# A local transformer on one core: probabilities divided by their sums on GpSimd, value products that give features by queries, the token shift by a transfer, and other orders of the engines' work

## What is computed

```python
def shift_tokens(t):
    a, s = jnp.split(t, 2, -1)
    s = jnp.pad(s, ((0, 0), (1, 0), (0, 0)))[:, :-1]
    return jnp.concatenate([a, s], -1)
...
def attn_layer(x, Wqkv, qs, ksc, Wo):
    q, k, v = jnp.split(x @ Wqkv, 3, -1)            # heads of 64
    ...
    q = l2norm(q) * qs
    k = l2norm(k) * ksc
    q = q * cos * scale + rotate_half(q) * sin * scale
    k = k * cos * inv + rotate_half(k) * sin * inv
    sim = jnp.einsum('bhwie,bhwje->bhwij', bq, bk2) * QK_SCALE
    sim = jnp.where(mask, -jnp.finfo(sim.dtype).max, sim)
    attn = jax.nn.softmax(sim, -1)
    out = jnp.einsum('bhwij,bhwje->bhwie', attn, bv2)
    return out @ Wo
...
for i in range(DEPTH):                              # 6
    x = attn_layer(shift_tokens(x), ...) + x
    x = ffn_layer(shift_tokens(x), ...) + x         # layer norm, 341 gated units, GELU
```

## Time and profile before

| | us |
|---|---|
| median of 3 runs | 2675.39 |
| range of the runs | 2669.9 to 2679.36 |
| the profiled execution | 2678.02 |
| its span, first to last instruction | 2676.1 |

### The profile page before, as it was taken

How to read it: one execution, slowest core, us unless ns; L and a number is a source line. 1 busy time by engine, 2 the same in 40 slices (tenths; PEclk the granted TensorE clock), 3 DMA queues, 4 the chain that set the end, 5 groups by cost and what they waited for, 6 DMA issues and landing times.

```text
span 2676.1 us, 103018 instructions
## 1 busy us (share of the span) xinstructions
PE 2507.1 (94%) x41090; PEld 1932.3 (72%) x41090; DVE 1977.9 (74%) x4815; ACT 1762.2 (66%) x3794; POOL 1492.9 (56%) x1917
## 2 busy tenths in 40 slices
PE   7879999999999999999999999999898978999898
PEld 5647677777767767777677767776677966899667
DVE  5777888888778788878788888887466877465564
ACT  5567777777777777777777777777344356333465
POOL 4567667666766766676667666775232146000472
PEclk9989999999999999999999999999799989899999
DMA  2200000111001100110011000000002000000022
GB/s 85 72 14 14 14 16 18 28 29 29 18 22 32 32 14 22 32 29 21 18 32 29 23 18 18 16 14 15 4 4 85 0 5 5 1 0 1 12 76 79
DMA packets 56280, 66.72 MB, mean 25 GB/s; under 512 B 25097, under 2 KB 30932, under 8 KB 55380
## 3 DMA queue, kind: packets, MB, share of 16 engines
q1 hardware_dynamic: 56148, 64.87, 8.7%
HBM read 38.23 MB, written 1.05 MB: 15 GB/s over the span
## 4 chain that ended last, share of the span: by engine, by line
PE 80%; DVE 6%; issue 5%; POOL 4%; ACT 3%; DVEq 1%; SPq 0%; POOLq 0%; DMA 0%; ACTq 0%
PE ps L795 13%; PE ps L900 6%; PE ps L816 6%; PE ps L809 6%; PE ps L880 5%; PE ps L843 5%; PE ps L922 4%; PE ps L857 3%; PE ps L1014 3%; PE ps L934 3%; PE ps L890 3%; PE ps L998 3%; PE ps L999 3%; ACT area L1190 2%; PE ps L738 2%
## 5 line engine op out<-in xcount | busy, mean ns | idle before, releaser
L1190 ACT ACTIVATE area<-ps 128x512 f32<-128x512 f32 (+3 forms) x1520 | 758.1, 532 | 415.9 <-PE ps L786 130.0
L1665 POOL TENSOR_TENSOR area<-area 128x512 f32<-128x512 f32 x384 | 482.2, 1277 | 7.9 <-DVE area L2164 7.9
L1687 POOL TENSOR_TENSOR area<-area,mx 128x512 f32<-128x512 f32 x192 | 200.2, 1043 | 491.1 <-DVE mx L2192 491.1
L795 PE MATMUL ps<-lw,area 128*128 128x512 f32 x768 | 414.1, 622 | 1.1 <-ACT area L1190 0.7
L1679 POOL TENSOR_TENSOR area<-area,rnq 128x512 f32<-128x512 f32 x384 | 393.2, 1046 | 7.5
L1313 ACT ACTIVATE area<-ps 128x512 f32<-128x512 f32 x384 | 227.4, 592 | 88.7 <-PE ps L795 88.6
L2162 DVE TENSOR_TENSOR area<-ps,table 128x512 f32<-128x512 f32 x384 | 261.0, 680 | 8.2 <-ACT area L1313 5.4
L2164 DVE TENSOR_TENSOR area<-ps,table 128x512 f32<-128x512 f32 x384 | 261.5, 681 | 0.0
L2143 DVE TENSOR_REDUCE ssq<-area 128x8 f32<-128x512 f32 x384 | 252.3, 677 | 2.4 <-ACT area L1313 1.5
L809 PE MATMUL ps<-ident,area 128*128 128x128 f32 x1536 | 218.6, 275 | 11.1 <-POOL area L1679 7.7
L809 PEld LDWEIGHTS ps<-ident,area 128*128 128x128 f32 x1536 | 180.7, 142 | 66.3 <-issue 54.3
(11 more groups left out here) (301 smaller groups left out, 5681.9 us busy)
## 6 DMA issues: line engine op xcount, KB each, us to landing
lvm<-area SPq DMA_DIRECT2D x384, 65.0 KB
lw<-in_wqkv SPq DMA_DIRECT2D x36, 256.0 KB
area<-in_moe_w SPq DMA_DIRECT2D x24, 256.0 KB, 2.8
lw<-in_wout SPq DMA_DIRECT2D x12, 256.0 KB
ctxT<-in_ctxT SPq DMA_DIRECT2D x64, 38.5 KB, 1.8
lw<-in_moe_w SPq DMA_DIRECT2D x8, 256.0 KB, 2.8
lw<-in_wff SPq DMA_DIRECT2D x6, 341.0 KB
lw<-in_moe_g SPq DMA_DIRECT2D x1, 1152.0 KB
```

The lines of the kernel that those rows point to most:

```text
L795: nc.tensor.matmul(banks[:, lb_qk[j], :], xsT[s], wqkv[w.p][:, j * 512:(j + 1) * 512], start=True, stop=True).then_inc(l_qk_ps, 1)
L1190: return nc.scalar.activation(dst, src, ACT.Identity if kw else ACT.Copy, **kw)
L1665: pool.tensor_tensor(QR[s][:, cols], QR[s][:, cols], RA[s][:, cols], ALU.add).then_inc(l_rsum, 1)
```

## The change

Five things change in the local transformer.

1. **Probabilities are divided before the value products.** `prob_sums` (VectorE, a reduction of 512 columns a half) and `inverse_sums` give the reciprocals, and `probs_normed` (GpSimd) multiplies the probabilities by them in place. `outputs` on VectorE is gone.
2. **`probs_values` gives features by queries.** Values are stationary (64 keys x 64 features), the transposed probabilities moving: for each pair of heads `c` query columns 0 to 63, 64 to 95 and 96 to 127, for the upper and the lower 64 rows in turn. That is 24 matmuls a half in two 64x64 tiles on the diagonal of the array, both into one PSUM bank. The result is already what `project` needs, so the transposes `outputs_T` on TensorE are gone; ScalarE copies straight from the products' bank.
3. **The shift of `y1` is a DMA transfer.** SyncE moves 127 rows x 64 features from `y1` one partition down into `ysh` beside it; VectorE reads columns 0 to 63 and 128 to 191 of `ysh`. `shift_back` and the constant `shift` are gone.
4. **New orders** of the work on TensorE, ScalarE, VectorE and GpSimd, and other PSUM banks. Values are projected by `values(*b, ...)`, no longer `values(*a, ...)`; the query and key blocks come in the order 2, 3, 0, 1; the transposes of queries and keys and the first scores of a unit now stand in its first step; `up` is split.
5. SyncE's transfers are issued per step by `stages`, with the shift behind the four middle transfers of the same unit.

```diff
             def probs_values(s, w, m):
...
                 for c in range(4):
-                    for n in range(4):
+                    for first, cols in ((0, 64), (64, 32), (96, 32)):
                         for odd in range(2):
-                            rows, out_rows = slice(64 * odd, 64 * odd + 64), slice(32 * n, 32 * n + 32)
-                            at = (4 * m + c) * S + 32 * n
-                            v = LVM[s][rows, 4 * m + c, :] if n == 2 else LV[s][rows, n // 2, 4 * m + c, :]
-                            last = nc.tensor.matmul(banks[out_rows, lb_pv[m][odd], c * 65:(c + 1) * 65],
-                                                    LPT[s][rows, at:at + 32], v, start=True, stop=True)
+                            rows = slice(64 * odd, 64 * odd + 64)
+                            at = c * S + first
+                            v = LVM[s][rows, 4 * m + c, 0:LD] if first == 64 else LV[s][rows, first // 64, 4 * m + c, 0:LD]
+                            last = nc.tensor.matmul(banks[rows, lb_pv[m], at:at + cols], v,
+                                                    LPT[s][rows, m * 512 + at:m * 512 + at + cols], start=True, stop=True)
...
-            def shift_back(s, w):
-                pe.wait_ge(l_y1, nth(0, w.it, s))
-                nc.tensor.matmul(banks[:, lb_shift, 0:64], ident[:, :], y1[s][:, 0:64], start=True, stop=True)
-                nc.tensor.matmul(banks[:, lb_shift, 64:128], shift[:, :], y1[s][:, 64:128],
-                                 start=True, stop=True).then_inc(l_sh_ps, 1)
...
+            def shifted_tokens(s, unit):
+                sp.wait_ge(l_y1, unit + 1)
+                sp.dma_start(ysh[s][1:S, D:D + 64], y1[s][0:S - 1, 64:D]).then_inc(l_sh_ps, 16)
+
+            def stages(a, b, c):
+                if a:
+                    middle_values(*a)
+                    shifted_tokens(*a)
...
+            def probs_normed(s, w, m):
+                if m == 1:
+                    pool.wait_ge(l_rc, nth(0, w.it, s, 2, 1))
+                P = heads8(LP[s], m)
+                pool.tensor_tensor(P, P, rc[s][:, 8 * m:8 * m + 8, None].to_broadcast([S, 8, 64]), ALU.mult).then_inc(l_o, 1)
...
+            def prob_sums(s, w, m):
...
+                V.tensor_reduce(sums[s][:, 8 * m:8 * m + 8], heads8(LP[s], m), AX.X, ALU.add).then_inc(l_psum, 1)
...
-            def outputs(s, w, m):
...
-                V.tensor_tensor(LO[s][:, m * 512:(m + 1) * 512].rearrange("p (c k e) -> p k c e", k=2, e=LD), pv(m)[:, :, :, 0:LD],
-                                per_head(rc[s][:, 8 * m:8 * m + 8])[:, :, :, None].to_broadcast([S, 2, 4, LD]), ALU.mult).then_inc(l_o, 1)
...
             def stages(a, b, c):
-                if a:
-                    values(*a, 0)
-                    values(*a, 1)
+                if b: values(*b, 0)
+                if a: tokens_T(*a)
+                if b: scores(*b, 1)
+                if a: queries_keys(*a, 2)
+                if b: values(*b, 1)
```

More of the change, by code:

```diff
@@ L554, in layer_and_next_weights @@
                             sp.dma_start(dst, src).then_inc(lw_loaded[p], 16)
-            layer(0)
+            stages((0, 0), None, None)
+            stages((1, 1), (0, 0), None)
+            with sp.Fori(0, IT - 1) as pr:
+                for s in range(G):
+                    three(s, pr * G + G + s)
             with sp.Fori(0, DEPTH // 2 - 1) as lp:
@@ L559, in _ @@
                 layer_and_next_weights(lp * 2 + 2, 1)
-            layer(DEPTH - 1)
+            with sp.Fori(0, IT) as pr:
+                for s in range(G):
+                    three(s, (DEPTH - 1) * B + pr * G + s)
+            stages(None, (1, DEPTH * B - 1), (0, DEPTH * B - 2))
+            stages(None, None, (1, DEPTH * B - 1))
             contexts(1)
```

357 lines of the change are left out of this document (174 added, 183 removed).

## The result

The changed kernel takes 2835.12 us (median of 4 runs, 2834.83 to 2839.52) against 2674.39 for the kernel before on the same chip: a ratio of 1.0601, 95% interval 1.058 to 1.0622. The prediction had the direction (slower) and was 102 us too fast: 2733 us, range to 2805.

What follows compares the result with a forecast made beforehand. TensorE, 94% busy, was taken as the bound. A step of 17.15 + 1.3 + 0.1 = 18.55 against 17.85 us, taken as +0.65, times 95 gave +62, drain -4: 2736, or 2733 us from the runs' median; range 2645 to 2805.

Steps and rivals of the forecast that it cites:

- What bounds the kernel, and that all lies in 95 steps: TensorE, 94% busy, bounds the kernel; the change lies wholly inside 95 local transformer steps of 17.85 us on average.
- Removed work, 1.46 us: TensorE's step loses two output transposes, 0.53 and 0.44 us, and the pair of shift matmuls, 0.49 us.
- Value products, 1.4 a half: In TensorE's step, 24 record pairs at 0.058 us take 1.4 us a half, before 0.79; two halves add 1.22 us.
- The second rival: Value products cost 0.79 to 0.86 us a half because weight loads run ahead; total 2633 us, chance 0.13.
- subtraction gives 17.15, I take 17.15: TensorE's own work a step: 17.39 - 1.46 + 1.22 = 17.15 us, a fall of only 0.24 us.
- The shift, one SyncE issue: Shift transfer between two units' middle transfers: issue about 0.6 us plus 1.8 to landing, VectorE asks some 3 us later; delays neither.
- GpSimd's slip: Divided probabilities come 5.9 to 6.6 us into the step, TensorE asks at 5.9; the middle transfers' wait absorbs the lateness.
- The wait for the middle transfers, 1.3: TensorE waits 1.3 us a step (1.1 to 2.6) ahead of the value products for four SyncE transfers of values.
- The token transpose, 0.1: Wait for VectorE's token copy behind a loop's branch: of 0.80 us about 0.2 remain every second unit, 0.1 on average.
- First rival, a shared PSUM bank: Two row tiles cannot write one bank together; a value-product half costs 1.7 to 2.8 us, total 2790 to 3000, chance 0.12.
- Third rival, transfers hidden anyway: TensorE reaches the value products late anyway or the landing is quicker; step 17.25 us, total 2615, chance 0.06.
- Fourth, GpSimd as the bound: GpSimd or VectorE becomes the bound behind the transfers' wait: +0.5 us a step, total 2780 us, chance 0.12.

Runs made afterwards that it cites:

- the transpose inside: The changed kernel with one more transpose of the tokens, its result unread, in the middle of the second scores' small-tile records: 2898.79 us, ratio 1.0842.

## Why the prediction was right or wrong, point by point

- **What bounds the kernel, and that all lies in 95 steps**: right; 155 of the 160 us.
- **Removed work, 1.46 us**: those rows are gone. **Value products, 1.4 a half**: 1.52. The 0.058 us a pair was exact; the 0.12 us to get out of the small tiles was left off. It makes +1.46 a step where I had +1.22. The reason I gave holds: two tiles go side by side, and in each the load of 64 columns sets the pace, every 0.058 us whether 64 or 32 columns are streamed. The second rival (products cheaper than their loads) is out.
- **The step that failed: "subtraction gives 17.15, I take 17.15."** I saw that the new order "enters and leaves tiles three times more", set against it that the removed pieces had stood beside tiles too, and priced both at zero. Work that is the same in both kernels takes about 0.54 us a step more in the new order. A split of the value projections alone costs 0.25 us (taken back in the changed kernel) to 0.38 (made in the kernel before). That much is shown; the remaining 0.16 to 0.29 is spread over other groups (0.07 of it stands just ahead of the transfer wait) and was only read, not tested. The Trainium skill, TensorEngine Tiling (Array Packing), Tiling Modes, says that "Mode switching requires drain". The traces show time lost at such changes, 0.13 us there and back for the small tiles of the scores and 0.25 to 0.38 for the half tiles of the projections; that a drain is what takes it, they do not show.
- **The shift, one SyncE issue, "delays neither"**: right in effect, by luck in the numbers. I had the landing 2.4 us after the issue began and VectorE asking some 3 us after the residual. The transfer takes at least 3.4 us, and VectorE asks 3.9 us after the issue; it waits in 3 of the 96 units. Asking at 3 us, as I had it, it would have waited 0.4 us in each.
- **GpSimd's slip "ends before the transfers do, so the wait absorbs it"**: right for the sum. 0.18 us of it stand ahead of the transfer wait and shorten that.
- **The wait for the middle transfers, 1.3**: 1.16, and 117 us by the run without them. The landing was right (3.86 us from the first issue to the last landing, median, where I had 3.8); TensorE's work ahead of the products is 4.58 us, not 4.3.
- **The token transpose, 0.1 for "a loop's branch"**: 0.15, by another cause. VectorE's copy is held while a GpSimd instruction runs (0.84 us in the changed kernel's step above); that the branch pushed it behind the start of one is likely, but not tested. The wait of 0.80 us in the kernel before came at 31 units, one in three, and not "at every second unit".
- The sum again with measured terms: 17.44 - 1.46 + 1.46 + 0.54 + 0.18 + 1.16 + 0.15 = 19.47, and 19.45 is the step. The miss of 0.99 us in TensorE's work is, to rounding, 0.54 for the same work in the new order, 0.24 for the products, 0.18 for the division's short waits and 0.05 for the base. Outside the steps the changed kernel's span grew by 1.5 us; the forecast had -4 there.
- **First rival, a shared PSUM bank**: refuted. The rule of the Trainium skill that I had quoted for it (same page, Restrictions and Gotchas) does not show in these times: two row tiles in one bank, writing different partitions, run at full overlap, and one after the other costs 1.2 us a half more.
- **Third rival, transfers hidden anyway**: not in the changed kernel; hidden by the order with both projections first, and then two other waits appear. **Fourth, GpSimd as the bound**: not while the transfers are there (a GpSimd 15 of 200 us lighter leaves the step unchanged); with the transfers covered it is the next wait, 0.5 us.
- **The range** took in the fourth rival and missed, because the work was one number without a spread: 17.0 by walking the order and 17.15 by subtraction were two ways of pricing tile changes at zero, not two measurements.

## What to carry to other kernels

Price the neighbours of a small-tile group as well as its records: subtract two places in the trace where the same records stand beside the same shape and beside another, and multiply by the entries and exits that the new order adds. A transfer that replaces a little TensorE work costs its place in a queue, its landing and whatever stands behind the instruction that waits, so look up all three before counting the matmuls saved. And when a wait is removed, walk to the next two late inputs; here both orders that covered the transfers turned one wait into another.

## What the runs showed of the hardware that was not expected

**VectorE held by GpSimd.** Beside the token copy (0.23 or 0.97 us, above), the small maximum over the sums of squares went from a mean of 237 ns to 531 ns in the changed kernel, where GpSimd has more to do:

```profile
L2151 DVE TENSOR_SCALAR ssq<-ssq 128x16 f32<-128x16 f32 x192 | 45.5, 237 | 6.6
```

```profile
L2157 DVE TENSOR_SCALAR ssq<-ssq 128x16 f32<-128x16 f32 x192 | 102.0, 531 | 3.3
```

(First the kernel before, then the changed one.) VectorE's sums and rotations keep their times in both. The Trainium skill, GPSIMD Engine Reference, Specifications, lists the SBUF interfaces as shared with VectorE, with contention for some of its instructions. The traces agree as far as two of VectorE's instructions are held in this way (0.97 against 0.23 us, 531 against 237 ns) and others are not.

**The clock.** Several kernels lost more than their waits. Windows of the kernel with the tokens on ScalarE, a long step and a stretch of it:

```profile
730.04:751.39 21.35, 19.51 (x302) 14.18 (x300) 14.39 (x30) 13.70 (x30) 14.09 (x16) 0.92 0.07 16
...
740.50:743.40 2.90, 2.90 (x24) 2.57 (x24) 1.92 (x4) 1.94 (x5) 1.16 (x2) 0.50 0.00 0
```

In the long step the granted clock is 0.50, that is 1.2 GHz, from about 740.5 on, although TensorE is busy throughout. Ahead of it, it had stood 1.35 us for the transfers and 0.4 for the scores, and two microseconds of products and transposes at full clock lie between. Each such stretch costs some 1.5 us of a step. In the changed kernel, with a transfer wait of 1.16 us, three of the 95 steps have one, the first two and one at 807 us, behind a single wait of 3.0 us. With 1.35 us it is 17 and 14 of 95 (the transpose inside, one head in eight divided), and 24 with both waits. At 1.5 us each that makes 26, 21 and 36 us. The length of this wait alone does not decide it: with one row tile after the other it is 1.16 us again, and 63 of the steps have such a stretch. Why some steps and not others is open.
